# Two cross attentions of a decoder kernel, reordered into rounds of two key tiles with 64-row mask products

## The reference

```python
scores = einsum('bhqd,bhkd->bhqk', Q, K) / sqrt(d_k)
scores = where(mask[:, None] == 0, -1e9, scores)      # layer 1
attn = where(context_mask[:, None, None, :], -inf, attn)   # layer 2, attn = scores
attn = softmax(attn, axis=-1)
Z = einsum('bhqk,bhkd->bhqd', attn, V)
return einsum('btd,ed->bte', Zc, Wo) + bo
```

## Time and profile before

| | |
|---|---|
| time, median of 3 runs | 6183.48 us (6180.24 to 6185.01) |
| span of the profiled execution | 6180.5 us |
| PE busy | 4319.4 us (70%) |
| DVE busy | 3667.5 us (59%) |
| ACT busy | 2628.5 us (43%) |
| POOL busy | 756.9 us (12%) |

### The profile page before, as it was taken

The page is one execution under the profiler, slowest core; times in us unless marked ns, Lnnn a source line. Parts: engine busy times, 40 slices in busy tenths (PEclk is TensorE's granted clock), DMA queues, the critical chain, the costliest instruction groups (busy, mean ns, idle before and its releaser), DMA issues. The chain is left out here.

```text
span 6180.5 us, 82959 instructions
## 1 busy us (share of the span) xinstructions
PE 4319.4 (70%) x31970; PEld 1559.0 (25%) x31970; DVE 3667.5 (59%) x7693; ACT 2628.5 (43%) x4771; POOL 756.9 (12%) x842
## 2 busy tenths in 40 slices
PE   5956999544699999999964899999877641134224
PEld 2333444333122222222242122222134320012011
DVE  5464666556877777777345998998724650137122
ACT  2522666224366666666611587888730110001001
POOL 0000000002000000000002000000000027722772
PEclk9878999767799999999976899999988875567567
DMA  0020000024000000000004001100014000000000
GB/s 13 1 62 10 15 11 9 15 100 155 18 12 10 3 12 12 12 12 1 1 6 104 1 12 19 17 12 12 1 15 147 13 5 13 12 5 5 13 13 8
DMA packets 119874, 141.87 MB, mean 23 GB/s; under 512 B 48269, under 2 KB 96620, under 8 KB 116846
## 3 DMA queue, kind: packets, MB, share of 16 engines
q1 hardware_dynamic: 77870, 118.15, 7.6%
q0 software_dynamic: 20480, 10.53, 1.1%
q10 hardware_dynamic: 21128, 7.88, 0.5%
HBM read 103.35 MB, written 33.14 MB: 22 GB/s over the span
## 5 line engine op out<-in xcount | busy, mean ns | idle before, releaser
L1480 ACT ACTIVATE probs<-ps 128x512 f32<-128x512 f32 x3264 | 1734.3, 598 | 763.0 <-PE ps L1425 762.9
L1515 DVE CUSTOM_DVE_ANT_0 junk<-ps,mask 128x512 bf16<-128x512 f32 (+1 forms) x1664 | 1049.1, 678 | 362.5 <-PE ps L1387 346.4
L1510 DVE TENSOR_REDUCE maxima<-ps 128x2 f32<-128x1024 f32 (+1 forms) x832 | 956.2, 1199 | 110.6 <-PE ps L1387 104.2
L1441 PE MATMUL ps<-probs,vstack 128*9 128x512 f32 x6528 | 873.0, 596 | 0.4 <-ACT probs L1480 0.4
L1425 PE MATMUL ps<-qturned,kturned 52*128 52x512 bf16 x3264 | 792.8, 385 | 83.7 <-ACT probs L1480 64.8
L1387 PE MATMUL ps<-kturned,qturned 49*128 49x512 bf16 (+1 forms) x3328 | 704.6, 392 | 110.8 <-DVE maxima L1510 35.7
L3172 POOL DMA_INDIRECT line<-table,index x640 | 644.8, 1008 | 876.9 <-DVE index L3545 483.5
L1418 PE MATMUL ps<-maskT,lower 128*128 128x512 fp8e5 x1632 | 562.3, 387 | 63.5 <-ACT probs L1480 15.1
L1425 PEld LDWEIGHTS ps<-qturned,kturned 52*128 52x128 bf16 x3264 | 196.2, 93 | 791.8 <-ACT probs L1480 462.1
L1387 PEld LDWEIGHTS ps<-kturned,qturned 49*128 49x128 bf16 x3328 | 166.3, 95 | 492.7 <-DVE maxima L1510 200.3
L1418 PEld LDWEIGHTS ps<-maskT,lower 128*128 128x128 bf16 x1632 | 123.5, 96 | 598.6 <-ACT probs L1480 433.4
(11 more groups left out here) (718 smaller groups left out, 4826.6 us busy)
## 6 DMA issues: line engine op xcount, KB each, us to landing
raw<-in_mask_BxSxS_if SPq DMA_DIRECT2D x8, 3202.0 KB, 13.2
kturned<-keys_parts SPq DMA_DIRECT2D x192, 102.0 KB
table<-lines SPq DMA_DIRECT2D x51, 256.0 KB, 3.0
line<-table,index POOLq DMA_INDIRECT x640
keys_parts<-parts SPq DMA_DIRECT2D x24, 384.0 KB, 2.7
vstack<-values_heads SPq DMA_DIRECT2D x16, 459.0 KB, 16.5
lose<-in_mask_SxS_bc SPq DMA_DIRECT2D x32, 128.0 KB
values_heads<-vall SPq DMA_DIRECT2D x2, 1728.0 KB, 10.4
```

Of the source, the lines that this page charges most:

```text
L1441: last = nc.tensor.matmul(k.ps[at:at + HD + 1, 3, :], vstack[:, p % 2, a, t, :], probs[:, (h * KT + t) % slots, a, :], start=(t < 2), stop ...
L1480: nc.scalar.activation(probs[:, u % slots, a, :], k.ps[:, (2 * u + a) % 3, :], ACT.Exp, scale=(1.0 if maskT is None else 1.0 / STEP8)).the ...
L1510: nc.vector.tensor_reduce(dst, ring(e).rearrange("p (a n) -> p a n", a=2)[:, :, 0:hi - lo], AX.X, ALU.max).then_inc(ring_free[at % 2], 1)
L1515: nc.vector.tensor_tensor_reduce(junk[:, at % 2, a * BANK:a * BANK + hi - lo], ring(e)[:, a * BANK:a * BANK + hi - lo], mask8[:, 4 * b + m ...
```

## The change

- Half h is now pair h % 8 and query half h // 8. Keys and values are loaded once per half, in two parts of keys (24 transfers) and four of values. Only 512 queries of the mask are kept turned, as bf16; those of the second query half are stored by `mask_turned` and loaded by `cross` during half 7 and after.
- The mask product is split by the array's rows: rows 0 to 63 write one bank, rows 64 to 127 another. A bank then holds 64 keys of both heads (128 partitions), and the scores of a unit are four products of 64 columns. `probs` of a unit is one exponential over 1024 columns. The values are stored 18 wide, with a block of zeros for the other head.
- A piece is one head only: 104 pieces in a half, each with one product, one bank and one VectorE operation, which is the maximum with a subtraction in both attentions (unmasked it subtracts a tile of zeros).
- PSUM: banks 0 to 3 for the scores of two units, bank 4 for weighing, banks 5 to 7 a ring of three slots of one bank.
- The order is in rounds of two units: masks of both, pieces, scores of both, weighing, pieces. `LEAD` goes from 3 pieces to 12.

```diff
-        vall = s.sb("vall", [P, H, KT, HD + 1])
+        vall = s.sb("vall", [P, H // 2, 2, KT, 2, HD + 1])
...
+                if g < 4:
+                    for a in range(2):
+                        nc.gpsimd.memset(vall[:, 2 * g:2 * g + 2, a, :, 1 - a, :], 0.0).then_inc(strips_cleared, 1)
...
-LEAD = 3
+LEAD = 12
 WEIGHS = KT // 2 + 1
+RING = 3
...
+    early = [c for c in range(len(CHUNKS)) if CHUNKS[c][1] <= EARLY * P]
+    rest = [c for c in range(len(CHUNKS)) if c not in early]
+    return [(m, c, a) for cs in (early, rest) for m in range(4) for c in cs for a in range(2)]
...
+    out = [("queries", 0)] + [("piece", 0, i) for i in range(n)] + [("queries", 1)]
+    out += [("piece", 1, i) for i in range(4)] + [("shifted", 0)] + [("piece", 1, i) for i in range(4, LEAD)]
+    spread = []
+    for h in range(HALVES):
+        parts = both_of(h + 1, LEAD, n) if h + 1 < HALVES else []
+        if h + 2 < HALVES:
+            parts += [[("queries", h + 2)]] + both_of(h + 2, 0, 4) + [[("shifted", h + 1)]] + both_of(h + 2, 4, LEAD)
+        elif h + 1 < HALVES:
+            parts += [[("shifted", h + 1)]]
+        cut = [-(-len(parts) * min(t, KT - 2) // (KT - 2)) for t in range(KT + 1)]
+        spread += [[e for part in parts[cut[t]:cut[t + 1]] for e in part] for t in range(KT)]
...
+    for g in range(HALVES * KT // 2):
+        out += [("masks", 2 * g)] + spread[2 * g] + [("scores", 2 * g)] + late.pop(g, []) + spread[2 * g + 1]
...
+            return k.ps[:, 5 + ring_at[e] % RING, :]
 
         def ring_wait(eng, e):
-            if ring_at[e] >= 2:
-                eng.wait_ge(ring_free[ring_at[e] % 2], ring_clear[e])
+            if ring_at[e] >= RING:
+                eng.wait_ge(ring_free[ring_at[e] % RING], ring_at[e] // RING)
...
+            def masks(u):
+                h, t = divmod(u, KT)
+                if u >= 2:
+                    pe.wait_ge(probs_ready, u - 1)
+                if h == PAIRS and t % KEPT == 0:
+                    pe.wait_ge(masks_loaded[t // KEPT], 16)
+                for first in range(2):
+                    mine = slice(64 * first, 64 * first + 64)
+                    nc.tensor.matmul(k.ps[:, 2 * (u % 2) + first, :], k.split[mine, :], maskT[mine, t, :],
+                                     start=True, stop=False, skip_group_check=True)
+
+            def score(u):
+                h, t = divmod(u, KT)
+                if maskT is None and u >= 2:
+                    pe.wait_ge(probs_ready, u - 1)
+                if t == 0:
                     read_wait(pe, ("shifted", h))
...
+                for first in range(2):
+                    for a in range(2):
+                        rows = slice(a * SLOT, a * SLOT + ROWS)
+                        to = slice(64 * (a ^ first), 64 * (a ^ first) + 64)
+                        last = nc.tensor.matmul(k.ps[to, 2 * (u % 2) + first, :],
+                                                kturned[rows, h % 2, t * P + 64 * first:t * P + 64 * first + 64],
+                                                qturned[rows, h % 3, :], start=maskT is None, stop=True, skip_group_check=True)
+                last.then_inc(scores_filled, 1)
...
+                        nc.scalar.activation(probs[:, u % slots].rearrange("p b n -> p (b n)"),
+                                             k.ps[:, bank:bank + 2, :].rearrange("p b n -> p (b n)"), ACT.Exp,
+                                             scale=(1.0 if maskT is None else 1.0 / STEP8)).then_inc(probs_ready, 1)
...
+                ring_wait(dve, e)
+                lost = nothing[:, 0:hi - lo] if mask8 is None else mask8[:, 4 * b + m, lo:hi].bitcast(mybir.dt.uint8)
+                nc.vector.tensor_tensor_reduce(junk[:, at % RING, 0:hi - lo], ring(e)[:, 0:hi - lo], lost, 1.0, -3.0e38,
+                                               ALU.subtract, ALU.max, maxima[:, h % 2, 4 * a + m, c:c + 1]).then_inc(ring_free[at % RING], 1)
```

More of the change, by code:

```diff
@@ L1223, with both_of, programme @@
 CHUNKS = [(a, min(a + BANK, SP)) for a in range(0, SP, BANK)]
-LEAD = 3
+LEAD = 12
 WEIGHS = KT // 2 + 1
+RING = 3
+PAIR = 2 * (HD + 1)
+KEPT = 10
+EARLY = 24
 def pieces():
-    return [(m, c) for m in range(4) for c in range(len(CHUNKS))]
-def programme(lag, masked):
-    n = len(pieces())
[L1236 to L1242, removed]
+    early = [c for c in range(len(CHUNKS)) if CHUNKS[c][1] <= EARLY * P]
+    rest = [c for c in range(len(CHUNKS)) if c not in early]
+    return [(m, c, a) for cs in (early, rest) for m in range(4) for c in cs for a in range(2)]
+def both_of(h, first, last):
+    return [[("piece", h, i), ("piece", h, i + 1)] for i in range(first, last, 2)]
+def programme():
+    n = len(pieces())
+    out = [("queries", 0)] + [("piece", 0, i) for i in range(n)] + [("queries", 1)]
[9 more added lines that the diff above has]
+        spread += [[e for part in parts[cut[t]:cut[t + 1]] for e in part] for t in range(KT)]
     late = {}
@@ L1245, in programme @@
         for i in range(WEIGHS):
[L1246 to L1258, removed]
+            late.setdefault((h * KT + min(2 * i + 1, KT - 1)) // 2 + 1, []).append(("weigh", h, i))
+        late.setdefault(((h + 1) * KT - 1) // 2 + 2, []).append(("sums", h))
+    for g in range(HALVES * KT // 2):
+        out += [("masks", 2 * g)] + spread[2 * g] + [("scores", 2 * g)] + late.pop(g, []) + spread[2 * g + 1]
+    for g in sorted(late):
+        out += late[g]
     return out
@@ L1382, in piece @@
+                if CHUNKS[c][0] == EARLY * P and m == a == 0:
+                    pe.wait_ge(keys_loaded[h % 2][1], 192 * (h // 2 + 1))
                 ring_wait(pe, e)
[L1383 removed]
                 lo, hi = CHUNKS[c]
[L1385 to L1388 removed]
@@ L1389, in piece @@
[L1389 to L1403 removed]
+                rows = slice(a * SLOT, a * SLOT + SHIFT)
@@ L1623, in mask_turned @@
     nc = k.nc
-    groups = [(t, range(a, min(a + 4, KT))) for t in range(NT) for a in range(0, KT, 4)]
+    fours = [range(a, min(a + 4, KT)) for a in range(0, KT, 4)]
+    groups = [(b, m, cs) for b in (1, 0) for cs in fours for m in range(4)]
     with Stage(nc) as s:
+        later = s.sb("later", [P, KT, BANK], BF16)
         turned = s.sem("turned")
```

320 lines of the change are left out of this document (159 added, 161 removed).

## The result

The changed kernel took 6326.09 us (median of 4 runs, 6322.72 to 6339.45) against 6184.24 (6180.24 to 6186.04): a ratio of 1.0235, 95% interval 1.0221 to 1.025. It is slower by 142 us. The forecast was 6287, its range 6050 to 6440.

A forecast was written before the change was run, and what follows sets the result against it. Before, TensorE bounds the masked cross, nothing by much the unmasked; after, a 3.00 us chain bounds both. Rounds -119 and +206, prologues -2, loads -16, `context_sides` +34: +103 on 6180.5, 6284, median 3 over: 6287 us, range 6050 to 6440.

The forecast's parts named there:

- The ring of A2, scores, weighing, B1, VectorE, slot: Round of two units, both crosses: a chain through TensorE and VectorE closed by the three ring slots, 3.00 us a round.
- A2: Second piece ahead of the scores in a round; claimed to need B1's slot, with TensorE standing 0.96 us there unmasked.
- B1: First piece behind the weighing in a round; VectorE starts on it after 0.43 us, its slot frees 0.75 later.
- Extra pairs: Five of 49 units in a half get a second pair of pieces: 1.22 us each, 6.1 us a half.
- Exponentials' chain, masked: Masked round: scores, two exponentials of 1024 columns, mask, pieces, scores again; 2.96 us, bounds 2.9 to 3.1.
- Masked rounds: Masked cross's rounds in sum: 1340 us against 1459, -119; 6 less since half 14 has no extras.
- Unmasked rounds: Unmasked cross's rounds in sum: 1291 us against 1085, +206; 6 less since half 14 has no extras.
- the clock as a rival of its own: Unmasked rounds: lower clock in a quarter of 408 rounds, each 1.2 us longer; +122 us, 6409; chance 0.10.
- Prologues: Work ahead of each cross's rounds, with 12 pieces of lead: 71 us in both, +3 masked and +7 unmasked.
- First loads and `context_sides`: Staging: smaller first loads save 8 us in each cross (-16); more fills and longer stores cost 17 each (+34).
- VectorE becomes the bound: Rival, both crosses: TensorE keeps ahead, a half takes 67.5 us, kernel about 5800; half-way cases 6050 to 6180; chance 0.18.
- Two after two: Rival: a unit's four score products run two at a time, 0.43 us more a round, kernel 6647; chance 0.06.

The follow-up runs named there:

- order experiment: Changed kernel with the two pieces ahead of the scores moved behind them in both crosses, nothing else changed: 5971.72 us, ratio 0.9651.
- short VectorE: Changed kernel with VectorE reading 256 of a piece's 512 columns in the unmasked cross alone: 6109.62 us, ratio 0.9874.
- missing masks: Changed kernel without the mask products in the masked cross: 6340.89 us, ratio 1.0255.
- early fill: Changed kernel with four useless products a round ahead of the first unit's scores in the unmasked cross, none in the last half: 6268.34 us, ratio 1.0139.
- the fill: Changed kernel with four useless 64-row products a round in the unmasked cross, placed as masks are in the masked one: 6316.16 us, ratio 1.0206.

## Why the prediction was right, and where it was off

The direction and the mechanism were right. Step by step:

- *The ring of A2, scores, weighing, B1, VectorE, slot.* Forecast 3.00 us in both crosses, measured 3.04 in both; the first unit's scores take 0.24 and not 0.22. The order experiment cuts it, the short VectorE shortens it by just the link's change, and the missing masks leave it as it was.
- *Extra pairs.* Forecast 1.22 on a round, measured 4.26 - 3.04 = 1.22.
- *Exponentials' chain, masked.* Forecast 2.96, level with the other. By the plain round above it is 2.46 + 0.22 + 0.32 = 3.00, just under the ring; in the reordered kernel, without the pieces in it, it is 2.78.
- *Masked rounds.* Forecast 1340 less 6 for half 14, measured 1339.8. Terms offset each other in it: 63 rounds have an added pair and not 75, some 15 us less than forecast, and other rounds are longer by somewhat more.
- *Unmasked rounds.* Forecast 1291 less 6, measured 1343.5, and 1287.4 with the clock held up. So the chain's part was right within 3 us, and the step that failed is the one that took the clock as a rival of its own with a chance of 0.10: it fell in addition. The prediction's price for it was 122 us, for a quarter of the rounds at 1.2 us; it was 56, for about a tenth at 1.3. The granted 0.93 is also under the 0.95 that it names as a sign of being wrong. The earlier trace rows have 0.99 and 1.00 in the rounds of before, which is why I gave it little; but they are rows of a TensorE that had more to do.
- *Prologues.* +10 forecast without half 14's part, +10.5 measured.
- *First loads and `context_sides`.* Forecast +18 together, measured about -8. The staging cost 9.6 and not 17 in the masked cross: the fills of 918 elements take 0.93 us, and I had scaled from 1.57 for 816; they were partly hidden too. The first loads gave 13 instead of 8, outside the bounds. How the 4.4 us between the crosses divide was not taken apart.
- *Rivals.* "VectorE becomes the bound" did not come true, for the reason given against it, that A2's wait stands in the order. With A2 behind the scores the unmasked round is 2.48, against VectorE's own 2.44. The prediction lets VectorE win where the run from A2 to B1 is under 1.26; in that kernel it is 1.30, so the rival is nearly reached there and not quite. Its price was too good besides, since the masked cross then hangs on the exponentials (1233 us instead of the 1085 that the rival gives). "Two after two" did not come true: eight products in 0.63 us, the second unit 0.24 behind the first.

The errors were +6 (masked), +58 (unmasked), -26 (loads and staging), +1 and -1 (the rest): +38, the distance of the two spans to each other (6322.4 against 6284). That the total came so near is in part luck: the overpriced loads and staging hide nearly half of the clock's 56 us.

## What to carry to other kernels

In an order that engines follow strictly, ask of each instruction that may wait what is queued behind it. Here a product that needs a slot stood ahead of the scores that feed another engine; moved behind them, with nothing else changed, it took 354 us off the kernel, some 50 of them by the clock that came back with it (an estimate from the 56 of the early fill). A change that makes one stage's engine time smaller should be read for the ring it builds: add up the links once round, and compare with the engines' own sums. If the ring is longer than all of them, time saved on an engine outside the ring is worth nothing, as with the mask products here. And a stage from which TensorE's work is taken can lose its clock, as two stages here did; useless products in the waits then gave 56 us back, and next to nothing where they had to wait for ScalarE themselves.

## What the runs showed of the hardware

- Four products of 64 columns lie on the four quarters of the array, and two of them, on different rows, write different partitions of one bank. All four run together: the eight of two units have starts and ends within 0.63 us (first fence of the timeline), and one unit follows the other after 0.24. Products that share rows (the two heads' are on separate ones, the two key halves of a head on the same) ran together too: a unit's four start within 0.01 us of each other. The Trainium skill, "TensorEngine Tiling (Array Packing)", Restrictions and Gotchas, says that different row tiles cannot access one PSUM bank at the same time. No run here shows a delay or a fault from it, for 6528 such products in the changed kernel.
- An exponential of 1024 columns takes 1.02 us and follows another after 0.92.
- The granted clock fell in rounds of 3.04 us without mask products (0.93 unmasked, 0.92 in the masked cross without masks) and stayed at 1.00 in rounds of the same length with them or with the fill, and at 0.99 or 1.00 in the shorter rounds without them (2.48 and 2.77 us). A stage that waits pays for the lower clock too: its round goes from 3.04 to 4.34 us, since scores and weighing are links of the chain.
